# An attention block and a two-group mixture of experts: kv kept in PSUM, a tile stage begun under the last scatters, and 16 experts split beside the attention steps

## The reference, cut to what matters

```
h   = layernorm(x) * (1 + ca) + sa
k,v,r = layernorm(h; gamma, beta) @ Wk.T, Wv.T, Wr.T
kv  = k * v
wkv = sigmoid(tf) * kv + td * shifted cumsum over t of (kv * td**t)     # td = sigmoid(time_decay)
x   = x + ga * ((sigmoid(r) * wkv) @ Wo.T)
h   = layernorm(x) * (1 + cb) + sb
out = x + gb * (moe_group_0(h) + moe_group_1(h)) / 2
moe_group: top 2 of 32 experts by softmax(h @ router), no token dropped;
           per expert (silu(h @ wg) * (h @ wu)) @ wd, weighted, summed per token   # 512 -> 256 -> 512
```

## Time and profile before

| | |
|---|---|
| median of three runs | 5099.27 us (5093.23 to 5112.04) |
| the profiled execution's own time | 5084.64 us |
| its span, first to last instruction | 5082.9 us |
| mean granted TensorE clock in it | 0.956 of 2.4 GHz |
| busy in the span | PE 4608.2 us, DVE 3209.4, POOL 2901.9, ACT 1634.6 |
| moved by DMA | 1152.42 MB, 227 GB/s in the mean |

### The profile page before, as it was taken

How to read it: one execution, slowest core, us unless ns; L and a number is a source line. 1 busy time by engine, 2 the same in 40 slices (tenths; PEclk the granted TensorE clock), 3 DMA queues, 4 the chain that set the end, 5 groups by cost and what they waited for, 6 DMA issues and landing times.

```text
span 5082.9 us, 89076 instructions
## 1 busy us (share of the span) xinstructions
PE 4608.2 (91%) x22649; PEld 3806.4 (75%) x22649; DVE 3209.4 (63%) x6155; ACT 1634.6 (32%) x4045; POOL 2901.9 (57%) x2301
## 2 busy tenths in 40 slices
PE   6999899999999982888888888998999999999998
PEld 4877777777778772767767776777788888888886
DVE  6999999999999993444444443454444444444443
ACT  2344444444434440222222322332222222222222
POOL 2577777777777774444444444454455555555554
PEclk8999999999999995999999998999999999999999
DMA  6545455555545453899999999998899999898887
GB/s 227 183 156 184 154 180 162 168 166 173 173 149 186 157 161 126 287 314 295 285 305 317 303 270 297 297 313 263 257 243 250 246 227 262 238 242 216 224 224 190
DMA packets 413885, 1152.42 MB, mean 227 GB/s; under 512 B 57057, under 2 KB 57058, under 8 KB 394930
## 3 DMA queue, kind: packets, MB, share of 16 engines
q0 software_dynamic: 182512, 454.27, 37.4%
q1 hardware_dynamic: 189634, 544.27, 30.5%
q10 hardware_dynamic: 41472, 151.01, 7.9%
HBM read 719.35 MB, written 463.57 MB: 233 GB/s over the span
## 4 chain that ended last, share of the span: by engine, by line
PE 33%; DMA 20%; issue 4%; POOL 2%; DVE 1%; POOLq 1%; SPq 0%; DVEq 0%; ACT 0%; ACTq 0%
DMA out<-c_yo,c_idx 19%; PE ps L1286 10%; PE ps L1288 9%; PE ps L1287 9%; PE ps L1295 3%; PE ps L1314 1%; POOL out L1277 1%; POOL c_xg L1246 1%; DVE c_yo L1530 1%; POOLq L1269 0%; DMA c_wt<-wsp_d 0%; DVE c_xl L1518 0%; DMA wsp_d<-c_stg 0%; DVE c_hTl L1523 0%; POOL c_lists L1258 0%
## 5 line engine op out<-in xcount | busy, mean ns | idle before, releaser
L1277 POOL DMA_INDIRECT out<-c_yo,c_idx x576 | 917.6, 1593 | 1075.5 <-DMA out<-c_yo,c_idx 592.9
L1286 PE MATMUL ps<-c_wt,c_xh 128*128 128x512 f32 x2304 | 966.3, 419 | 40.9 <-issue 22.6
L1288 PE MATMUL ps<-c_wt,c_xl 128*128 128x512 f32 x2304 | 910.4, 395 | 0.0
L1287 PE MATMUL ps<-c_wt,c_xh 128*128 128x512 f32 x2304 | 906.4, 393 | 0.0
L1530 DVE SCALAR_TENSOR_TENSOR c_yo<-ps,c_wc,c_xg 128x512 f32<-128x512 f32 x576 | 432.5, 751 | 707.9 <-DMA out<-c_yo,c_idx 444.6
L1246 POOL DMA_INDIRECT c_xg<-h2g_d,c_idx x576 | 573.2, 995 | 508.9 <-DVE c_yo L1530 396.5
L1514 DVE TENSOR_TENSOR c_hh<-ps,c_sil 128x256 f32<-128x256 f32 x576 | 244.0, 424 | 842.8 <-ACT c_sil L1366 788.7
L431 PE MATMUL ps<-xTh,wTh 128*128 128x512 f32 x1536 | 625.9, 407 | 106.1 <-DVE xTl L800 91.1
L1371 ACT CAST c_xh<-ps 128x512 fp32r<-128x512 f32 x576 | 337.7, 586 | 1101.9 <-PE ps L1295 1037.1
L693 POOL DMA_INDIRECT list_d<-pairs,sidx x512 | 568.2, 1110 | 213.9 <-issue 132.5
L1286 PE MATMUL ps<-c_wt,c_hTh 128*128 128x512 f32 x1152 | 468.7, 407 | 168.6 <-DVE c_hTl L1523 159.6
(11 more groups left out here) (196 smaller groups left out, 8074.7 us busy)
## 6 DMA issues: line engine op xcount, KB each, us to landing
c_wt<-wsp_d SPq DMA_DIRECT2D x69, 2048.0 KB
c_wt<-wsp_d SPq DMA_DIRECT2D x69, 1024.0 KB
sraw<-wex SPq DMA_DIRECT2D x194, 256.0 KB
wsp_d<-shigh SPq DMA_DIRECT2D x192, 256.0 KB
wsp_d<-sraw SPq DMA_DIRECT2D x192, 256.0 KB
c_stg<-wex ACTq DMA_DIRECT2D x96, 512.0 KB
wsp_d<-c_sgh ACTq DMA_DIRECT2D x96, 512.0 KB
wsp_d<-c_stg ACTq DMA_DIRECT2D x96, 512.0 KB
```

Source lines behind the costliest of these rows:

```text
L1277: nc.gpsimd.indirect_dma_start(out=out, out_offset=bass.IndirectOffsetOnAxis(ap=idx[:, n:n + 1], axis=0), in_=yo[:, n % 4, :], in_offset=N ...
L1286: nc.tensor.matmul(o, lh, rh, start=first, stop=False)
L1287: nc.tensor.matmul(o, lh, rl, start=False, stop=False)
L1288: return nc.tensor.matmul(o, ll, rh, start=False, stop=last)
```

## The change

It has three parts.

1. **kv stays in PSUM.** DVE writes kv back into the v bank and wk into the k bank; the scan and the wkv operation read them there. ACT's biased k goes straight into `aa`, which wkv later overwrites. `cs` gets a row for each chunk and carries its own last column, so the copy of the total goes. A k bank is now free after the scan, a v bank after wkv.
2. **The tile stage begins under the last scatters.** The last step's 16 list scatters move from the end of the first stage to the start of POOL's program in the second, in front of the list gathers, which wait for them. `ranks(B, 0)` and `place(B, -2)` go ahead of the output product and the residual, and most scatters of the last but one step are issued earlier. The tile stage gets its slot numbers from setup and fills `odd` on DVE; one POOL iota is left there, behind the list gathers. PE transposes the expert order first, and SP starts the weight loads on it, before the lists are in. The first transposes of tile rows no longer wait for the wait counts.
3. **16 experts of group 1 are split in the first stage**, two in each batch row: 10 jobs in a step in place of 7. The low parts of jobs 4, 5 and 6 of each step are taken on DVE (`DVE_LOW`), the other seven on POOL. In the second stage 16 experts are left, one in every two turns.

```diff
-JOBS = 28
-PER_STEP = 7
+JOBS = 40
+PER_STEP = 10
+DVE_LOW = (4, 5, 6)
...
             else:
                 dc = next(i for i in range(KC) if q0 in PROJ[i])
-                who, m, v = (k_biased, kv_ready, r_sig)[PROJ[dc].index(q0)], 4, dc + 1
+                who, m, v = (scan, wkv_ready, r_sig)[PROJ[dc].index(q0)], 4, dc + 1
...
                 def turn(i):
                     j = s * PER_STEP + i
-                    if i % 2 == 0:
+                    if i % 2 == 0 and i < 8:
                         spread_gate(b, s * 4 + i // 2)
...
+                turn(3)
+                turn(4)
                 if not (first and s == 0):
                     store_x1(b, s - 1)
-                turn(3)
-                if not (first and s == 0):
                     store_h2(b, s - 1)
...
-                turn(4)
-                turn(5)
-                turn(6)
+                for i in range(5, PER_STEP):
+                    turn(i)
...
+            ranks(B, 0)
             output(B, 0)
-            ranks(B, 0)
             back(B, 0)
...
             def chunk_k(b, s, dc):
                 act.wait_ge(proj_done, cnt(b, s, 12, 3 * dc + 1))
-                wait(act, kv_ready, cnt(b, s, 4, dc))
-                nc.scalar.activation(kb[:], bank(s, PROJ[dc][0]), ACT.Identity,
+                wait(act, s_ready, cnt(b, s, 4, dc - 1))
+                nc.scalar.activation(aa[:, dc % 2, :], bank(s, PROJ[dc][0]), ACT.Identity,
                                      bias=bias[:, 0, dc:dc + 1]).then_inc(k_biased, 1)
...
                 normed(b, s)
+                stage_hi(b, at + 4)
                 chunk_k(b, s, 1)
+                stage_hi(b, at + 5)
                 chunk_r(b, s, 1)
...
                 hi(b, s, 1)
-                stage_hi(b, at + 4)
+                stage_hi(b, at + 6)
                 chunk_r(b, s, 2)
                 chunk_k(b, s, 3)
                 hi(b, s, 2)
-                stage_hi(b, at + 5)
+                stage_hi(b, at + 7)
                 if back_too:
                     logits(b, s)
-                stage_hi(b, at + 6)
+                stage_hi(b, at + 8)
+                stage_hi(b, at + 9)
                 front(b, s, (0, 1))
...
                 receive(b, s, 2)
-                stage_lo(b, at + 4)
+                if old:
+                    scatter(b, s - 2, 8, 9)
                 lo(b, s, 2)
-                stage_lo(b, at + 5)
-                stage_lo(b, at + 6)
+                stage_lo(b, at + 7)
+                stage_lo(b, at + 8)
                 if old:
-                    scatter(b, s - 2, 8, 10)
+                    scatter(b, s - 2, 9, 10)
+                stage_lo(b, at + 9)
                 receive(b, s, 3)
...
+            scatter(B, -3, 11, 16)
+            scatter(B, -2, 0, 6)
             rstd(b_var, vab, h2_ready, rsb, b_rstd, B, -1)
-            scatter(B, -3, 11, 16)
-            scatter(B, -2, 0, 16)
-            scatter(B, -1, 0, 16)
+            scatter(B, -2, 6, 16)
...
             def chunk(b, s, dc):
-                u = dc % 2
+                kb, kv, wk = aa[:, dc % 2, :], bank(s, PROJ[dc][1]), bank(s, PROJ[dc][0])
...
-                V.scalar_tensor_tensor(out=wk[:], in0=kv[:], scalar=gs[:, dc, s:s + 1],
+                V.scalar_tensor_tensor(out=wk, in0=kv, scalar=gs[:, dc, s:s + 1],
                                        in1=pw[:, dc, :], op0=ALU.mult, op1=ALU.mult).then_inc(wk_ready, 1)
...
-                V.tensor_tensor_scan(cs[:, 1:TT + 1], ones[:, 0:1].to_broadcast([P, TT]), wk[:],
-                                     cs[:, 0:1], ALU.mult, ALU.add).then_inc(scan, 1)
+                V.tensor_tensor_scan(cs[:, dc, 1:TT + 1], ones[:, 0:1].to_broadcast([P, TT]), wk,
+                                     cs[:, dc, 0:1], ALU.mult, ALU.add).then_inc(scan, 1)
                 dve.wait_ge(scan, cnt(b, s, 4, dc + 1))
-                V.tensor_copy(total[:, dc:dc + 1], cs[:, TT:TT + 1]).then_inc(totaled, 1)
-                wait(dve, s_ready, cnt(b, s, 4, dc - 1))
-                V.scalar_tensor_tensor(out=aa[:, u, :], in0=kv[:], scalar=tfc[:, dc:dc + 1],
-                                       in1=cs[:, 0:TT], op0=ALU.mult, op1=ALU.add).then_inc(wkv_ready, 1)
+                V.scalar_tensor_tensor(out=aa[:, dc % 2, :], in0=kv, scalar=tfc[:, dc:dc + 1],
+                                       in1=cs[:, dc, 0:TT], op0=ALU.mult, op1=ALU.add).then_inc(wkv_ready, 1)
...
+                stage_lo(b, s * PER_STEP + 4)
                 chunk(b, s, 1)
+                stage_lo(b, s * PER_STEP + 5)
                 chunk(b, s, 2)
+                stage_lo(b, s * PER_STEP + 6)
                 norm_front(b, s + 2, 0)
                 chunk(b, s, 3)
...
+            for i in range(sidx.shape[2]):
+                nc.gpsimd.indirect_dma_start(
+                    out=list_d, out_offset=bass.IndirectOffsetOnAxis(ap=sidx[:, 1, i:i + 1], axis=0),
+                    in_=pairs[:, 1, i, :], in_offset=None).then_inc(placed, 16)
             list_rows = list_d.rearrange("(r n) c -> r (n c)", n=P)
             pool.wait_ge(listed, 1)
+            pool.wait_ge(placed, 16 * sidx.shape[2])
...
             pe.wait_ge(t_exp, 1)
-            pe.wait_ge(t_must, 1)
             turn_x(0, 0)
...
-            turn(0, splitting=True, first=True)
-            with act.Fori(1, E - 1) as it:
-                turn(it, splitting=True)
-            turn(E - 1, splitting=True)
-            with act.Fori(E, NIT - 1) as it:
+            pair(0)
+            with act.Fori(1, EC - 1) as x:
+                pair(x)
+            pair(EC - 1)
+            with act.Fori(2 * EC, NIT - 1) as it:
                 turn(it)
```

More of the change, by code:

```diff
@@ L111, in jout, with lows @@
     return b * (SPLITS // 2 * 32) + n * 32
+def lows(b, j):
+    row, at = (0, j) if j >= 0 else (-1, j + JOBS)
+    own = [i for i in range(JOBS) if (i % PER_STEP in DVE_LOW) == (at % PER_STEP in DVE_LOW)]
+    n = row * len(own) + sum(i <= at for i in own)
+    return b * len(own) + n
 PARTS = ((0, 2048), (512, 2560), (1024, 3072), (1536, 3584), (4096, 5120), (4608, 5632))
@@ L1329, in turn @@
                     gate_up(it, s)
+                    if first and s == 0:
+                        pe.wait_ge(t_read, 1)
                     if not (first and s == 0):
@@ L1334, in turn @@
                     turn_h(it, s)
+            pe.wait_ge(listed, 1)
+            for c in range(COLS):
+                last = nc.tensor.transpose(ps[0:1, 4 + c // 4, c % 4 * P:(c % 4 + 1) * P], eidx[:, c:c + 1], ident[:])
+            last.then_inc(t_done, 1)
             pe.wait_ge(l_in, 16 * COLS)
@@ L1403, in turn, with pair @@
                     weight(it, s)
[L1404 to L1412 removed]
+                    if x is not None:
+                        m = half * 8 + s
+                        if m in (0, 5, 10):
+                            split_hi(x, m // 5)
+                        if m in (2, 7, 12):
+                            split_out(x, m // 5)
+                        if m in (5, 10, 15) and not (isinstance(x, int) and x == EC - 1):
+                            split_in(x + 1, m // 5 - 1)
+            def pair(x):
+                turn(x * 2, x=x, half=0)
+                turn(x * 2 + 1, x=x, half=1)
             for k in range(3):
@@ L1430, in _, with flat @@
             n = [0]
+            emin = cand[0:1].rearrange("p c n -> p (c n)")
+            emax = odd[0:1]
+            meet = lists[0:1].rearrange("p c n k -> p (c n k)").rearrange("p (a n) -> p a n", a=2)
+            n1 = COLS * P - 1
+            def flat(k):
+                return ps[:, 2 * k:2 * k + 2, :].rearrange("p a b -> p (a b)")[:, 0:COLS * P]
             def link(ins):
@@ L1531, in weigh, with split_lo, turn @@
                                        in1=xg[:, s % RING, C:2 * C], op0=ALU.mult, op1=ALU.mult).then_inc(y_ready, 1)
-            def stage_lo(it, k):
-                dve.wait_ge(stg_hi, job(it, k))
+            def split_lo(x, k):
+                dve.wait_ge(stg_hi, job(x, k))
                 V.tensor_tensor(stg[:, k].bitcast(F32R), stg[:, k], sgh[:, k].bitcast(F32), ALU.subtract).then_inc(stg_lo, 1)
-            def turn(it, first=False, splitting=False, final=False):
+            def turn(it, first=False, final=False, x=None, half=0):
                 for s in range(8):
@@ L1544, in turn, with pair @@
                     hlo(it, s)
-                    if splitting and s in (0, 3, 6):
-                        stage_lo(it, s // 3)
+                    m = half * 8 + s
+                    if x is not None and m in (0, 5, 10):
+                        split_lo(x, m // 5)
+            def pair(x, first=False):
+                turn(x * 2, first=first, x=x, half=0)
+                turn(x * 2 + 1, x=x, half=1)
             find_lists()
@@ L1551, in _ @@
             xlo(0, 1)
-            turn(0, first=True, splitting=True)
-            with dve.Fori(1, E) as it:
-                turn(it, splitting=True)
-            with dve.Fori(E, NIT - 1) as it:
```

(5 more changed lines are left out.)

162 lines of the change are left out of this document (79 added, 83 removed).

## The result

The changed kernel takes 4909.6 us in the median of four runs (4896.6 to 4915.0), the kernel before 5098.3 (5093.2 to 5112.0): ratio 0.962, 95% interval 0.959 to 0.965. The forecast was 4855 with a range of 4765 to 4945. The time lies in the range, 55 us above the likeliest, 10 us from the 4900 of rival B, in which the steps gain nothing. The profiled execution took 4905.7 us with a span of 4904.0; its clock was 0.971. One execution of one experiment, the profiled one of e10, ran at a granted clock of 0.555 and took 7643 us, where e10's other four took 4962 to 4973, so no row of e10 is used.

What follows compares the result with a forecast made beforehand. Prediction: DVE bounds the attention steps, DMA the first 256 tiles, PE the rest. Gains of 45 (steps), 30 (between stages), 150 (splits) and 8 (SP's wait) sum to 233 us, from 5084.6 to 4852; median put at 4855, range 4765 to 4945.

Steps and rivals of the forecast that it cites:

- rival B: Steps gain nothing: DVE's subtractions cost 1.54 us each and ACT's last cast holds the copies 0.5 us; 4900 us, chance 0.22.
- the 5 and 15 us: Widening of the range from 4770 to 4930 to 4765 to 4945, for bounds of the steps and between the stages.
- C: Tile stage: the first 256 tiles become PE-bound at 4.78 us, 85 us more gain; 4770 us, chance 0.17.
- D: Tile stage: the adds into `out` keep the pace and the tile gain is 75 us; 4930 us, chance 0.12.
- The saving on VectorE: Attention steps: kv and wk in PSUM shorten wkv, wk and scan, with the small copy gone; 5.1 us a step.
- PE is no bound for that, since 57.2 - 3.0 is above 52.2: Attention steps: PE's floor, 52.2 us, stays below the 57.2 us step even after DVE's upper net saving of 3.0.
- the later bank frees: Attention steps: BACKT+2 and +3 wait for chunk 1's scan and wkv; 1 us possible, costed at nothing.
- part 3's price in a step: Attention steps: three DVE subtractions at 1.117 us each, 3.4 us, and 0.3 us for ACT's later casts.
- If ACT's waits for `wsp_d` stores grow beyond 4 us a step: Attention steps: a sign that the forecast is wrong, set at ACT's store waits above 4 us a step.
- Between the stages: 30 forecast: Between first and tile stage: scatters leave the way, weights are asked for earlier, lists become the limit; 30 us, bounds 20 and 38.
- The tiles: 158 forecast: Tile stage: half the splits give 5.12 us a tile at DMA share 0.96, 150 us, plus 8 for SP's wait.
- Rival E: Attention steps: casts of jobs 8 and 9 wait for stores ahead of the xTh copies; slower, 5156 us, chance 0.04.

Runs made afterwards that it cites:

- e10: The changed kernel with VectorE's statistics of the step after next moved behind chunk 3 and split_x; 4970 us, ratio 0.980.
- e5: The changed kernel with VectorE's subtractions of split jobs, those not of wo, cut to 8 of 512 columns; 4908 us, ratio 0.962.
- e2: The changed kernel with three shigh buffers instead of two, so a cast waits for the third split job's store before it; 4904 us, ratio 0.962.
- e1: The kernel before with only the first part of the change, kv and wk in PSUM banks; 5053 us, ratio 0.992.
- e12: e2 with VectorE's subtraction of the fifth job behind chunk 1, where it stood ahead of it; 4883 us, ratio 0.964.
- e9: The changed kernel with the edits of e2 and e5 together; 4871 us, ratio 0.961.
- e11: e10 with the tenth job's cast also behind the xTh copies and last hi, its subtraction behind the last lo; 4937 us, ratio 0.974.
- e8: The changed kernel with the last 16 scatters issued at the end of the first stage, as before; 4930 us, ratio 0.965.
- e7: The changed kernel with the last part of the first stage in its old order; 4925 us, ratio 0.965.
- e4: The changed kernel without the 16 splits of the tile stage, tiles reading other experts' weights; 4848 us, ratio 0.952.

## Why the range held and the forecast for the steps did not

The sum was 54 us too high: 39 in the steps and 28 in the tiles, less 13 that came between the stages. The time lies in the range since the bounds of the steps began at 0, not since their mechanism held. That rival B's 4900 is so near is luck in part: its gain of the steps is right, its reasons are not shown (the three subtractions cost 3.8 us and not 4.6, and e5 and e2, which reduce them and the waits of the casts, are without effect alone). And the 5 and 15 us by which the range goes beyond C and D follow from no sum in the forecast.

**The steps: 45 us forecast, 6 measured.** The saving on VectorE was right (5.1 forecast, 5.5 measured), without any price for writing PSUM. Three things failed after it.

First, the step "PE is no bound for that, since 57.2 - 3.0 is above 52.2". In the earlier trace rows TensorE was busy 1382 of 1488 us, and its own waits there were 106 us, 4.0 a step: its work was 53 us, not the 51.5 that the forecast added up, and everything it could gain at that clock was those 4. And not all of them shrink with VectorE's work: in e1 VectorE stands idle for 81 us ahead of kv, and TensorE still waits 22 us for xTl and 21 for the scan; the step is 56.3.

Second, "it delays nothing on DVE, so I cost it at nothing" of the later bank frees. The wait of 1 us was foreseen in size (34 us in 26 steps are 1.3 each) and mispriced: it falls on TensorE, whose time it is, and with the longer transposes it is 1.5 a step. The forecast named the condition, "without PE's slack (57.2 against 52.2) it would be 1 us a step", and that is the case that holds. In e12 an earlier chunk 1 moved 14 us of it to the next bank. That it would all be gained if the banks were freed as before wasn't tried.

Third, part 3's price in a step was 3.4 + 0.3 us on VectorE and ScalarE, paid out of a saving of 5.1; the measured price is 33 us of 39 over the steps (e1 against after), about 1 us a step. The forecast took a mean for the subtraction, 1.12 us; there are two kinds, 0.68 and 2.8 us, and the dear one stands on the way to xTl. Cutting the columns brings nothing by itself (e5), nor does ending ScalarE's waits for stores (e2), which had grown to 8 us a step; with both, TensorE's wait for xTl falls from 42 to 24 us (e9). But it falls in e11 and e12 too, to 13 and 28, with the subtractions whole, and all three ran on the faster chips. How much of the 33 us e9 gives back is between 8 (by the ratio) and all of it (by the times as they stand), and in e9 the dear subtraction is still there. The cause of the 33 us stays open between these.

Of the forecast's signs of being wrong, "if PE waits in `back`" came true. "If ACT's waits for `wsp_d` stores grow beyond 4 us a step" was no sign: before the change they were 123 us in 26 steps, 4.7 each.

**Between the stages: 30 forecast, 42.7 measured**, above the bound of 38. Taking the scatters out of the way is worth 15 (e8), about half of what I had, and the reordered tail, which stands in the diff and which the forecast passed over, is worth 12 (e7). That the lists become the limit was right.

**The tiles: 158 forecast, 130 measured.** The mechanism was right, the size off in one term. 5.12 us a tile came from a DMA share that stays at 0.96 and a pace of 4.78 without splits. The share fell to 0.93, and the pace without any splits is 4.94 in this stretch (e4): half way from 4.94 to 5.71 is 5.32, and 5.23 was measured. From tile 3 to tile 255 the gain is 119 us (1442.2 against 1323.5) where the forecast had 150. SP's wait for the last split, 8 in the forecast, is worth 13; before, tile 256 came 17.6 us behind tile 255, and now 5.0:

```profile
3515.26 0.42 DVE L1514 TENSOR_TENSOR c_hh<-ps,c_sil 128x256 f32<-128x256 f32 x1 [14.58 <-ACT c_sil L1366]
```

Behind that the two kernels differ by 1 us. The waits for the adds into `out` did what rival D describes, in part: 356 us before, 210 after, 60 with no splits. That these waits end with the splits is not in the earlier trace rows, to which the forecast puts it; the trace before has 16.5 us of them on VectorE from 3700 to 4800 us. Rival E, the slower one, needed 6.2 us a step from ScalarE's casts: they wait 8 us a step for stores, but these waits don't lie in front of xTh alone, and TensorE's wait for xTl fell.

Of the two rules that the forecast cites, the one of the Trainium skill's DMA: Bandwidth & Descriptors (section SWDGE vs HWDGE vs iDMA) was to put the gain between the stages at 20 us; it is 42.7, and no run shows packets waiting for others. The one of the Trainium skill's VectorE: DVE Perf Modes (section The TRN2 errata), 62 cycles or 65 ns more for an instruction that reads PSUM, doesn't show here: the same operation of 128x512 takes 746 ns wholly on SBUF (L868) and 751 to 759 with an input in PSUM (L840, L825, L833), 5 to 13 ns more.

## What to carry to other kernels

When an engine that is 97% busy gets relief, look at the next one's waits before counting the gain: busy 93% with 4 us of waits a step means that 4 us is all there is at that clock, and e1 got 1.2 of them. A value kept in PSUM is paid for in the release of its bank, on the engine that wants the bank next; price that wait as time of that engine, not as slack. In a queue written out by hand, moving work out of a gap (the statistics ahead of chunk 3) can cost more than the wait that it cures, and two causes that hide each other have to be removed together before either is judged. When an experiment cuts an instruction's work, look in its trace whether the instruction became short: in e9 one in each step did not, and in e5 most of these.

## What was new of the hardware

On VectorE, `scalar_tensor_tensor` of 128x512 with an input in PSUM takes 750 to 760 ns in the mean in every kernel that keeps kv in PSUM, with the output in PSUM or SBUF. In the changed kernel 60 of the 104 of L840 lie beside a GpSimd computation, and the longest took 753 ns. The scan from PSUM takes 1280 ns. Before, the wkv operation (L827) had all its large inputs in SBUF: its 30 instances without a GpSimd computation beside them took 740 to 754 ns, the other 74 took 1.5 to 2.6 us, and each of these ended 0.55 us behind GpSimd's operation. So PSUM isn't faster as such; what it saves is this wait.

The wait doesn't depend on how much VectorE has to do. A subtraction of 8 columns on SBUF took 0.16 us alone and 2.4 to 2.6 us where GpSimd did two operations one right after the other (26 of 26 in e9); a whole one took 0.68 us alone and 2.9 to 3.1 in that place (26 of 26 in e2). VectorE didn't get in between the two.

Two of the four chips of the experiments ran the kernel before in 5071 us, the other two in 5099 and 5102.
